# Where the norms and query projections of a first cross-attention are made, in a two-layer decoder kernel

## The reference

```python
x = x + attn(layernorm(x))            # 16 heads of 64, softmax, output projection
x = x + xattn(layernorm(x), context)  # 16 heads of 8, rotated queries and keys
x = x + moe(layernorm(x))             # router to 2 of 16 experts, and shared experts
# layer 1: attention with relative positions, cross-attention, dense experts
```

## Time and profile before

| what | value |
|---|---|
| median of 3 runs | 1402.18 us (1400.52 to 1410.3) |
| the profiled execution's own time | 1399.95 us |
| its span in the trace | 1398.2 us |
| TensorE busy | 1257.2 us (90%) |
| VectorE busy | 969.2 us (69%) |
| ScalarE busy | 712.8 us (51%) |
| GpSimd busy | 617.3 us (44%) |

### The profile page before, as it was taken

One profiled execution on the slowest core, in us unless ns is written; L12 is line 12 of the kernel. 1 busy time (PEld: TensorE's weight loads), 2 busy tenths in 40 slices (PEclk: granted clock), 3 DMA queues, 4 the chain that ended last, 5 costly groups with the idle time before them and its releaser, 6 DMA issues.

```text
span 1398.2 us, 29260 instructions
## 1 busy us (share of the span) xinstructions
PE 1257.2 (90%) x10872; PEld 920.3 (66%) x10872; DVE 969.2 (69%) x2337; ACT 712.8 (51%) x1473; POOL 617.3 (44%) x756
## 2 busy tenths in 40 slices
PE   8999999999999779860749988989999999989998
PEld 5667676777777546540437656767777777767887
DVE  5988877777777678768413466666777888776554
ACT  4566666666666536620103335655666666633222
POOL 3565555555555311120541348685565655402110
PEclk9999999999999979965879999999999999999999
DMA  5131000000000100000013123211120210000001
GB/s 182 48 122 32 1 1 1 1 1 2 1 1 1 52 18 2 2 1 0 6 46 106 50 53 114 59 41 38 39 54 24 47 45 25 8 1 0 1 0 30
DMA packets 77000, 43.88 MB, mean 31 GB/s; under 512 B 26089, under 2 KB 71738, under 8 KB 76870
## 3 DMA queue, kind: packets, MB, share of 16 engines
q1 hardware_dynamic: 72342, 38.56, 10.4%
q10 hardware_dynamic: 2480, 2.29, 0.5%
q0 software_dynamic: 2048, 1.27, 0.4%
HBM read 21.89 MB, written 10.49 MB: 23 GB/s over the span
## 4 chain that ended last, share of the span: by engine, by line
PE 68%; DVE 16%; POOL 5%; ACT 4%; issue 4%; SPq 2%; DMA 1%; ACTq 0%; POOLq 0%; DVEq 0%
PE psum L1270 8%; PE psum L1255 7%; PE psum L1649 7%; PE psum L1245 6%; PE psum L1758 6%; PE psum L1769 4%; PE psum L1661 4%; PE psum L1633 3%; PE psum L1640 3%; PE psum L1481 3%; PE psum L1221 2%; POOL xs_rows L658 2%; PE psum L1279 2%; DVE negmax L2438 2%; SPq L571 2%
## 5 line engine op out<-in xcount | busy, mean ns | idle before, releaser
L606 POOL TENSOR_TENSOR arena<-arena,rden 128x512 f32<-128x512 f32 x256 | 260.6, 1040 | 209.9 <-DVE rden L1920 209.8
L893 ACT ACTIVATE arena<-psum,negmax 128x512 f32<-128x512 f32 x256 | 175.0, 692 | 150.9 <-DVE negmax L1911 131.6
L1911 DVE TENSOR_REDUCE negmax<-psum 128x1 f32<-128x512 f32 x256 | 168.0, 681 | 55.5 <-PE psum L1245 54.9
L2438 DVE TENSOR_REDUCE negmax<-psum 128x1 f32<-128x512 f32 x256 | 164.4, 684 | 53.1 <-PE psum L1640 51.1
L1255 PEld LDWEIGHTS psum<-cst,arena 128*128 128x128 f32 x1024 | 113.1, 141 | 44.7 <-issue 44.3
L1255 PE MATMUL psum<-cst,arena 128*128 128x128 f32 x1024 | 138.1, 276 | 3.1 <-DVE arena L1906 0.8
L1633 PE MATMUL psum<-a_kstack,a_qblk 96*128 96x512 f32 x256 | 96.5, 458 | 13.4 <-DMA a_kstack<-a_klo 8.6
L1245 PE MATMUL psum<-a_qk 64*128 64x512 f32 x768 | 106.0, 407 | 2.5 <-DVE a_qk L1929 2.5
L1758 PE MATMUL psum<-f_h,f_w 128*128 128x512 f32 x384 | 101.3, 414 | 7.0 <-DVE arena L2536 6.9
L1142 ACT ACTIVATE arena<-psum 128x512 f32<-128x512 f32 x64 | 38.1, 597 | 108.3 <-PE psum L1758 108.3
L1245 PEld LDWEIGHTS psum<-a_qk 64*128 64x128 f32 x768 | 67.4, 184 | 38.9 <-issue 24.2
(11 more groups left out here) (350 smaller groups left out, 2718.8 us busy)
## 6 DMA issues: line engine op xcount, KB each, us to landing
w<-in_ew SPq DMA_DIRECT2D x2, 2048.0 KB, 8.2
a_kstack<-a_khi SPq DMA_DIRECT2D x64, 64.0 KB, 2.0
xs_rows<-f SPq DMA_DIRECT2D x3, 1024.0 KB, 5.3
arena<-xs_rows SPq DMA_DIRECT2D x8, 384.0 KB, 3.7
ys_rows<-wqkv SPq DMA_DIRECT2D x8, 384.0 KB, 2.6
a_kstack<-a_klo SPq DMA_DIRECT2D x32, 64.0 KB, 2.0
a_kstack<-a_khi SPq DMA_DIRECT2D x64, 32.0 KB, 1.9
a_qstack<-a_qhi SPq DMA_DIRECT2D x120, 16.0 KB
```

Of the source, the lines that this page charges most:

```text
L606: pool.tensor_tensor(a0_p[u % 4], a0_p[u % 4], rden[:, u:u + 1].broadcast_to([P, SEQ]), ALU.mult).then_inc(a0_norm, 1)
L893: act.activation(a0_p[u % 4], bank[u % 4][:, :], ACT.Exp, bias=negmax[:, u:u + 1], accum_out=den[:, u:u + 1]).then_inc(a0_exp, 1)
L1911: dve.tensor_reduce(negmax[:, u:u + 1], bank[u % 4][:, :], AX.X, ALU.max, negate=True).then_inc(a0_max, 1)
L2438: dve.tensor_reduce(negmax[:, n % 8:n % 8 + 1], bank[n % 4][:, :], AX.X, ALU.max, negate=True).then_inc(a1_max, 1)
```

## The change

Three more guests enter A0: the norms of X0 for batches 0, 1 and 2 (numbers 4, 5, 6, turned in pairs 13, 21 and 29). The output bias for these batches is added by GpSimd at the start of the pair after the turn. TensorE projects their queries at the end of A0, interleaved with the last value products and ahead of the last output product. VectorE rotates the queries of batches 0 and 1 before the last `a0_add`. Batch 3's norm becomes like the guests of X0: scale by VectorE before tile 0, rounds and rows by GpSimd, turn and projection by TensorE in turn t = 2; its rotation comes after the shift of tile 2, and batch 2's after the shift of tile 0. `norm_layer` goes on all engines. In the router the last output product comes ahead of the turn of batch 2 and of the logits of batch 1, one filler matmul stands in place of three, and VectorE makes the last norm before it copies the first logits.

```diff
-        NORM_TURN = {4: 1, 7: 2, 10: 3}
+        NORM_TURN = {4: 1, 7: 2, 10: 3, 13: 4, 21: 5, 29: 6}
# GpSimd
+            def residual_bias(b):
+                xb = X[:, b * QT:(b + 1) * QT, :]
+                pool.tensor_tensor(xb, xb, bcast(x0bo[:, :], 1, QT), ALU.add).then_inc(pre_pool, 1)
             for g in range(PAIRS):
+                if g - 1 in NORM_TURN and NORM_TURN[g - 1] >= B:
+                    pool.wait_ge(ld_x0, 144)
+                    pool.wait_ge(ln_ready, NORM_TURN[g - 1] + 1)
+                    residual_bias(NORM_TURN[g - 1] - B)
...
-            pool.wait_ge(ld_x0, 144)
-            for b in range(B):
-                pool.wait_ge(ln_ready, X0 * B + b + 1)
-                xb = X[:, b * QT:(b + 1) * QT, :]
-                pool.tensor_tensor(xb, xb, bcast(x0bo[:, :], 1, QT), ALU.add).then_inc(pre_pool, 1)
...
+            batch_norm(B - 1, 1, ln_ready)
+            residual_bias(B - 1)
             for b in range(B - 1):
-                batch_norm(b, NT + b + 1, ln_ready)
+                batch_norm(b, b + 2, ln_ready)
# ScalarE
-            norm_layer(X0, ACT.Exp)
...
             for t in range(1, NT):
+                if t == 2:
+                    turned_tokens(2 * B - 1)
# TensorE
+            def x0_queries(b):
                 pe.wait_ge(ln_out, X0 * B + b + 1)
                 for i in range(2):
                     mm = pe.matmul(bank[2 * b + i][:, :], x0w[:, i, :], hT[:, b * SEQ:(b + 1) * SEQ], start=True, stop=True)
                 mm.then_inc(x0_q, 1)
+            x0_queries(0)
+            a0_values(PAIRS - 1, 0)
+            x0_queries(1)
+            a0_values(PAIRS - 1, 1)
+            x0_queries(2)
+            a0_output(PAIRS - 1)
...
             for t in range(1, NT + 4):
                 if t < NT:
                     x0_scores(t)
+                if t == 2:
+                    turn_tokens(2 * B - 1, ln_h[:, NT - QT:, :])
...
-                        for b in range(B - 1):
-                            f0_turn(b)
+                        f0_turn(0)
+                        f0_turn(1)
                         f0_router(0)
                     if 0 < u <= NT // 2:
                         x0_output(u - 1)
                     if u == NT // 2:
                         f0_router(1)
+                        f0_turn(2)
                         f0_router(2)
-                        keep_busy(bank[5], 3)
+                        keep_busy(bank[5], 1)
...
+                if t == 2:
+                    x0_queries(B - 1)
# VectorE
-            def a0_tokens(b, step):
-
+            def tokens(n, step):
+                b = n % B
                 if step == 0:
-                    dve.wait_ge(ld_xb[b], 16)
+                    if n < B:
+                        dve.wait_ge(ld_xb[b], 16)
+                    else:
+                        dve.wait_ge(a0_x, (b + 1) * HP)
...
-            a0_add(PAIRS - 1)
-            dve.wait_ge(a0_x, PAIRS)
-
-
-            for t in range(NT):
-                norm_stats(t)
-            norm_layer(X0)
...
-            for b in range(3):
-                x0_rope(b)
+            x0_rope(0)
+            x0_rope(1)
+            a0_add(PAIRS - 1)
+            dve.wait_ge(a0_x, PAIRS)
+            for t in range(NT - QT, NT):
+                norm_stats(t)
+            guest_scale(B - 1)
             for t in range(NT + 4):
                 if t < NT:
                     x0_shift(t)
-                if t == 1:
+                if t == 0:
+                    x0_rope(2)
+                if t == 2:
                     x0_rope(3)
...
             last_scale()
+            last_norm()
             logits(0, NT - QT, 0, 1)
-            last_norm()
```

More of the change, by code:

```diff
@@ L431, in scale_count @@
         def scale_count(kind, b):
-            return NT + B + [SCALE_AT[at] for at in sorted(SCALE_AT)].index((kind, b))
+            return B + 1 + [SCALE_AT[at] for at in sorted(SCALE_AT)].index((kind, b))
         def a1_from(i):
@@ L836, in warm @@
                 warmed[0] += 1
[L838 to L845, removed]
             for i, n in enumerate(("wq", "wk", "wv")):
@@ L854, in _, with turned_tokens @@
             warm(ACT.Exp)
-            def a0_tokens(b):
-                act.wait_ge(ln_tp, A0 * B + b + 1)
-                act.activation(hT[:, b * SEQ:(b + 1) * SEQ], bank[4 if b == 0 else 7][:, :], ACT.Copy).then_inc(ln_out, 1)
+            def turned_tokens(n):
+                b = n % B
+                act.wait_ge(ln_tp, n + 1)
+                act.activation(hT[:, b * SEQ:(b + 1) * SEQ], bank[7 if n else 4][:, :], ACT.Copy).then_inc(ln_out, 1)
             def context_values():
@@ L899, in a0_first_half @@
                 if g in NORM_TURN:
-                    a0_tokens(NORM_TURN[g])
+                    turned_tokens(NORM_TURN[g])
                 a0_exp_of(g, 0)
@@ L925, in a0_second_half @@
                     context_values()
-            a0_tokens(0)
+            turned_tokens(0)
             a0_copy_q(0)
@@ L996, in _ @@
                 f0_tokens(b)
-            act.wait_ge(ln_var_ok, F0)
+            act.wait_ge(ln_var_ok, 1)
             act.activation(ln_std[:, NT - QT:], ln_var[:, NT - QT:], ACT.Sqrt).then_inc(ln_std_ok, 1)
@@ L1182, in keep_busy, with turn_tokens @@
                         pe.matmul(o, ident, cst[:, 0:SEQ], start=True, stop=True)
[L1184 to L1194, removed]
+            def turn_tokens(n, rows):
+                pe.wait_ge(ln_ready, n + 1)
+                if n in NORM_FTC:
+                    pe.wait_ge(a0_ftc, NORM_FTC[n])
                 for t in range(QT):
-                    mm = pe.transpose(bank[4 if b == 0 else 7][:, t * P:(t + 1) * P], a0_h[:, t, :], ident)
+                    mm = pe.transpose(bank[7 if n else 4][:, t * P:(t + 1) * P], rows[:, t, :], ident)
                 mm.then_inc(ln_tp, 1)
@@ L1213, in _ @@
             pe.wait_ge(ld_id, 16)
-            a0_tokens(0)
+            turn_tokens(0, a0_h)
             def a0_project_q(g):
@@ L1286, in a0_first_half @@
                 if g in NORM_TURN:
-                    a0_tokens(NORM_TURN[g])
+                    turn_tokens(NORM_TURN[g], a0_h)
                 if g:
@@ L1330, in _ @@
             a0_turn_t(PAIRS - 1, 7)
-            a0_values(PAIRS - 1, 0)
-            a0_values(PAIRS - 1, 1)
-            a0_output(PAIRS - 1)
-            norm_layer(X0)
-            for b in range(B):
+            def x0_queries(b):
                 pe.wait_ge(ln_out, X0 * B + b + 1)
@@ L1824, in norm_stats @@
                 dve.bn_stats(st, xt).then_inc(ln_stat, 1)
-            def norm_layer(layer):
-                dve.wait_ge(ln_stat, counted[0])
-                for t in range(NT):
[L1830 to L1843, removed]
             def context_keys():
@@ L1891, in a0_tokens @@
                 if step in (3, 4):
-                    if b and step == 3:
-                        dve.wait_ge(ln_tp, A0 * B + b)
+                    if n and step == 3:
+                        dve.wait_ge(ln_tp, n)
                     for t in range(step % 3 * 2, step % 3 * 2 + 2):
@@ L1900, in _ @@
             for step in range(5):
-                a0_tokens(0, step)
+                tokens(0, step)
             def a0_copy(g, u):
@@ L1950, in a0_first_half @@
                 if 2 * g in NORM_AT:
-                    a0_tokens(*NORM_AT[2 * g])
+                    tokens(*NORM_AT[2 * g])
             def a0_second_half(g):
@@ L1966, in a0_second_half @@
                 if 2 * g + 1 in NORM_AT:
-                    a0_tokens(*NORM_AT[2 * g + 1])
+                    tokens(*NORM_AT[2 * g + 1])
             a0_low_q(0)
@@ L2073, in last_norm @@
                 last = slice(NT - QT, NT)
-                dve.wait_ge(ln_std_ok, F0)
+                dve.wait_ge(ln_std_ok, 1)
                 ln(dve.reciprocal(ln_rstd[:, last], ln_std[:, last]))
```

## The result

The changed kernel takes 1389.85 us (median of 11 runs, 1387.79 to 1397.62), the kernel before 1405.53 us beside it (11 runs, 1400.52 to 1411.19). The ratio is 0.9899, with a 95% interval of 0.9879 to 0.9918: faster by 1.0%, and the interval reaches to both sides of 1%. The same code was timed twice more: 0.9927 (0.9902 to 0.9952) and 0.9904 (0.9871 to 0.9937). The profiled execution took 1388.52 us (its span is 1386.7 us), 11.4 us less than the 1399.95 us of the one before. The forecast was 1390.1 us, and 1387.9 us for the profiled execution. The forecast counts from a median before of 1402.18 us, so as a ratio it is 0.9914, which lies inside the interval. That the absolute time is met within 0.3 us is partly luck, for the kernel before measured 1405.53 us this time.

The account below looks back on a forecast made before the run. TensorE bounds the first attention; at the seam a chain of VectorE work, turns, projections and rotations does. +5.7 + 0.1 - 14.5 - 3.4 = -12.1 us, giving 1390.1 against the median 1402.18; range 1383.5 to 1398.5.

Parts of the forecast that it names:

- The guests, +5.7: First attention: three new guest norms lengthen it by 1.9 us each, 5.7 us; 29.5 us if fully exposed.
- The bias, +0.1: Output bias on GpSimd before a pair's first division: hidden in a 1.67 us gap, +0.1 us, range 0 to 3.8.
- The first seam, -14.5: From attention to cross-attention: first maxima 17.5 us earlier, part given back, gain 14.5 us, bounds 12 and 16.5.
- The give-back by rotation, turn and projection: Cross-attention start: batch 2's rotation and batch 3's turn, projection and rotation reduce the 17.5 us to 14.5.
- the step-by-step walk: Cross-attention start: four engines followed from 490.3 with old durations, scores of tile 4 at 510.8 instead of 525.32.
- The router, -3.4: End of cross-attention: earlier output product, rows and last turn gain 3.4 us, range 2.5 to 4.3.
- the reason named with the term: Router: the last turn and logits behind it may run at the lower clock, costing back up to 1 us.
- The sum: Whole kernel: guests, bias, first seam and router add to -12.1 us, 1387.9 for the profiled execution.
- A: Guests and clock: guests nearly free (3 us), no clock loss, seam 16, router 4.3; -17.3 us, 1384.9; chance 0.2.
- B: First seam: TensorE's clock stays low behind it, costing 6.5 us, so -5.6 and 1396.6; chance 0.1.
- D: First seam: semaphore order holds early projections or batch 3's rows back; seam gain 8, near 1396.6; chance 0.09.
- C: First attention: VectorE's guest work exposed, slower from 6.0 us per guest, up to +11.6 us, 1413.8; chance 0.06.

Follow-up runs that it names:

- Experiment 6: Changed kernel without the Newton rounds of the three new guests, so their rows are scaled wrongly; ratio to the kernel before 0.9914.
- experiment 7: Changed kernel with the three bias additions on GpSimd behind the last pair instead of in pairs 14, 22 and 30; ratio to the kernel before 0.9915.
- experiment 1: Changed kernel run again with no edit; ratio to the kernel before 0.9927.
- experiment 4: Changed kernel with five filler matmuls behind the scores of tile 0, where TensorE idles; ratio to the kernel before 0.9899.

## Why the prediction was right

**The guests, +5.7.** They cost 5.1 us (457.49 less 452.36), 1.7 each instead of 1.9. The middle pitch is the old guest's (14.98); the last one is 0.48 over the plain pair, where the old third guest had 0.72. Why that one was dearer was not traced. The work was the same in the same kind of pair, contention with GpSimd included: a four-element instruction of the rounds takes 651 ns on average beside it, as in the earlier trace rows. The prediction set this beside an aggregate, another operation; the better measure is the same instruction with GpSimd idle, at the kernel's start, and there it takes 0.16 us (the section on the hardware has the rows). The page "GPSIMD Engine Reference" of the Trainium skill (Specifications) states that the two engines share their SBUF interfaces, with contention for VectorE's instructions with two SBUF inputs among others. The trace agrees: the instruction of the 651 ns has two. Experiment 6 shows how far it reaches: of some 3.7 us of rounds in a guest 0.56 us shows in the pitch, so the contention is mostly hidden.

**The bias, +0.1.** Nothing, shown by experiment 7.

**The first seam, -14.5.** The first maxima are 12.4 + 5.1 = 17.5 us earlier on the old clock, as worked out. The give-back by rotation, turn and projection was expected at 3.0 us by the scores of tile 4; it was 2.2 (525.47 less 515.22 is 10.25, and 5.13 for the guests makes 15.4), and another 0.8 went by the end, since the division stands 9.4 us ahead, 14.5 with the guests. So the sum was met and its course differed a little: TensorE waits once more for ScalarE behind the scores of tile 4 (0.93 us at 516), which the step-by-step walk had not followed. Two differences of 0.8 us cancel here, and that is luck.

**The router, -3.4.** It was 2.65 us in the first profile, 2.1 in the second and 2.5 in the third. The term was too large by about 1 us. The last turn came 3.1 us earlier (10.15 less 7.05) and not 3.7 to 4.3, because the logits ahead of it ran at the lower clock (1.89 us) and the filler took 2.05 us where 0.9 to 1.8 was allowed; the last turn started 1.35 us behind the last norm. The turn itself gave back another 0.45, for the reason named with the term, and in the second profile the last logits 0.8 more. The clock was what the term had wrong: in the two profiles that kept it full the router gains 4.7 us (12.65 less 7.97), over the upper bound.

**The sum.** By these marks the profiled gain is 12.05 us at the last logits against 12.1 forecast. The term of the guests was 0.6 us too dear and the router's 0.75 too large, so here too two misses cancel. The 11.4 of the whole execution is a near hit partly by luck: behind the marks it lost 4.5 us in the gaps of experiment 1 and got back about 4, at places where the code is the same and which were not traced. The other two profiles of the same code have spans of 1387.5 and 1382.9 us.

**The rivals.** A did not come: its guests (3 us) are too cheap against the measured 5.1, though a router gain above its 4.3 appeared in two experiments. B was right that the clock falls behind the first scores (0.50 from 498 to 504), and wrong on the price: by experiment 4 it costs 0.3 to 0.8 us, not 6.5, because VectorE sets the pace there. The page "TensorE: Matmul & The Clock Gate" of the Trainium skill, Part 1, has the low level as the default and activity as what releases it. The trace agrees: with fillers in TensorE's wait the clock stayed at 1.00. D did not occur: batch 3's rows were ready at 501.4 and TensorE took them at 505.3. C would have needed 6 us per guest.

## What to carry to other kernels

A norm that stands between two stages can go into the stage before, one batch at a time, as soon as that batch's last addition is made; price it by the lengthening of a loop turn that already holds such a guest, for that number contains the contention. At a seam, ask which engine's work sets the pace when the waits are gone: here it was VectorE's, and neither the order of TensorE's projections nor its clock mattered much. Where an engine's clock varies, compare marks inside the stage that was changed, for single executions differ by more elsewhere than the change is worth.

## What the runs showed of the hardware

The spread of one kernel's runs goes largely with TensorE's clock. Over 37 runs of the kernel before, times from 1390.7 to 1410.0 us go with mean granted clocks from 0.955 to 0.940, 0.9 us for each 0.001, with a correlation of -0.90. A profile shows such a place: the same instructions between tiles 3 and 4 at 0.50 or 1.00, worth 3 us; and the router's last turn and logits at either level, worth up to 2.6 us (10.58 against 7.97). Part of it has a visible cause: without a filler the clock fell in all three profiles within TensorE's 1.2 us wait for the last norm, and with one it did not fall there in the two that came to it at full clock. What makes it fall at 593 in one execution and not in another stays open.

A small VectorE instruction beside GpSimd is either short or held. In the changed kernel's first new guest:

```profile
191.67 2.04 POOL L614 TENSOR_TENSOR arena<-arena,rden 128x512 f32<-128x512 f32 x2 [0.18 <-DVE rden L1901]
...
191.83 0.90 DVE L1854 SCALAR_TENSOR_TENSOR ln_new<-ln_new,ln_rstd 128x4 f32<-128x4 f32 x1
192.77 0.96 DVE L1855 SCALAR_TENSOR_TENSOR ln_rstd<-ln_new,ln_rstd 128x4 f32<-128x4 f32 x1
```

Each of the two ends within 0.03 us of the end of a division of GpSimd (two of about 1 us each, from 191.67 to 193.71). At 186.43, with GpSimd idle, the same L1854 takes 0.16 us, as it does at the kernel's start (6.23). So it is with L1854 and L1855 in all six guests of this kernel: the 18 that begin during a division take 0.89 to 0.97 us and end with it within 0.03 us, and the 18 that begin with GpSimd idle take 0.16 or 0.17. So the 651 ns of the earlier trace rows is a mean of 0.16 and 0.9 us.

The gaps of up to 2.4 us in TensorE's issue appeared in one of twelve profiles of kernels with a part of the change or all of it. GpSimd issued its scatters beside the same product in all of them, so the scatters alone do not make the gaps. I did not find their cause.
